# Gated cross attention with a mixture of experts: relative and causal terms of the edge tiles on PE instead of DVE and GpSimd

## The reference

```
x = x + tanh(g_xattn) * attention(ctx, ctx, layernorm(x))     # x: 4 x 1024 x 256, ctx: 4 x 154 x 256, 16 heads of 16
x = x + tanh(g_ffn)   * experts(layernorm(x))                 # 8 experts of 128, 4 chosen by token, and a shared one

# attention, for one batch and head; queries q = 0..1023, keys k = 0..153
scores = (qh @ kh.T) + bias[q, clip(q - k, -4, 4) + 4]        # bias = qh @ p_params
scores = where(q >= k, scores, -1e30)
out    = softmax(scores) @ vh                                  # then @ Wo.T
```

## Time and profile before

| | |
|---|---|
| median of 3 runs | 729.9 us (727.46 to 731.66) |
| profiled execution | 729.36 us, span 727.3 us |
| PE busy | 617.1 us, 85% of the span |
| DVE, ACT, POOL busy | 458.1, 275.9, 177.3 us |
| first score of the attention | 61.9 us |
| last unit of the attention starts | 334.1 us |
| experts' dense stretch starts | 393.9 us |
| mean granted TensorE clock | 0.938 |

### The profile page before, as it was taken

How to read it: one execution, slowest core, us unless ns; L and a number is a source line. 1 busy time by engine, 2 the same in 40 slices (tenths; PEclk the granted TensorE clock), 3 DMA queues, 4 the chain that set the end, 5 groups by cost and what they waited for, 6 DMA issues and landing times.

```text
span 727.3 us, 10637 instructions
## 1 busy us (share of the span) xinstructions
PE 617.1 (85%) x3384; PEld 484.7 (67%) x3384; DVE 458.1 (63%) x884; ACT 275.9 (38%) x501; POOL 177.3 (24%) x177
## 2 busy tenths in 40 slices
PE   3665968797977977878667999999999999999997
PEld 2544734566544755554345888888888888888886
DVE  3577657868387768751277575756557475755653
ACT  2433356334643465334351322333242333324222
POOL 2151005300341006100010232232324223232222
PEclk9966989999999999889959999999999999999999
DMA  7750233524144333473122112031222202121220
GB/s 235 209 122 23 45 75 87 124 50 98 39 116 93 74 82 84 110 211 99 31 47 82 37 60 86 2 102 43 87 58 73 72 5 97 43 87 59 74 73 29
DMA packets 39856, 58.65 MB, mean 81 GB/s; under 512 B 7984, under 2 KB 21040, under 8 KB 39792
## 3 DMA queue, kind: packets, MB, share of 16 engines
q1 hardware_dynamic: 39824, 58.25, 29.3%
HBM read 31.76 MB, written 4.85 MB: 50 GB/s over the span
## 4 chain that ended last, share of the span: by engine, by line
issue 44%; POOL 5%; PE 1%; DVE 1%; POOLq 0%; ACT 0%; DVEq 0%
POOL hl L1165 4%; PE work L948 1%; POOL rstd L1159 0%; DVE stats L1246 0%; PE py L1462 0%; POOLq L1163 0%; DVE x L1346 0%; DVE xn L1256 0%; POOL veps L1157 0%; PE oT L937 0%; PE oT L933 0%; DVE mv L1250 0%; DVE at L671 0%; POOLq L1164 0%; POOLq L1156 0%
## 5 line engine op out<-in xcount | busy, mean ns | idle before, releaser
L1165 POOL TENSOR_TENSOR hl<-sg,hh 128x512 fp32r<-128x512 f32 x72 | 93.1, 1293 | 249.0 <-ACT hh L1208 249.0
L503 ACT ACTIVATE ex<-sT 128x512 f32<-128x512 f32 (+1 forms) x160 | 91.9, 593 | 157.2 <-PE sT L913 132.6
L1202 ACT ACTIVATE sg<-pg 128x512 f32<-128x512 f32 x72 | 43.0, 597 | 199.0 <-PE pu L1447 198.2
L872 PE MATMUL smax<-km,qs 96*128 96x308 f32 (+1 forms) x244 | 86.9, 392 | 26.7 <-DVE mx L604 19.3
L604 DVE TENSOR_REDUCE mx<-smax 128x2 f32<-128x308 f32 x185 | 81.1, 472 | 36.3 <-PE smax L872 35.1
L872 PEld LDWEIGHTS smax<-km,qs 96*128 96x128 f32 x244 | 49.0, 211 | 60.5 <-DVE mx L604 34.0
L1462 PE MATMUL py<-wxl,hh 128*128 128x256 f32 x288 | 81.8, 284 | 3.3 <-DVE x L1346 2.1
L1462 PE MATMUL py<-wxh,hl 128*128 128x256 f32 x288 | 80.8, 281 | 0.0
L1462 PE MATMUL py<-wxh,hh 128*128 128x256 f32 x288 | 80.5, 280 | 0.0
L1334 DVE TENSOR_TENSOR sg<-cwb,sg 128x512 f32<-128x512 f32 x64 | 66.9, 1045 | 10.8 <-DMA cwb<-cwt_d 7.9
L1329 DVE TENSOR_TENSOR sg<-pu,sg 128x512 f32<-128x512 f32 x72 | 49.2, 684 | 28.3 <-ACT sg L1202 27.0
(11 more groups left out here) (154 smaller groups left out, 1120.7 us busy)
## 6 DMA issues: line engine op xcount, KB each, us to landing
cwb<-cwt_d SPq DMA_DIRECT2D x64, 256.0 KB, 3.4
qs<-qh SPq DMA_DIRECT2D x64, 128.0 KB, 2.5
qs<-ql SPq DMA_DIRECT2D x32, 128.0 KB, 2.6
at<-rden_d SPq DMA_DIRECT2D x64, 64.0 KB, 2.3
out<-x SPq DMA_DIRECT2D x8, 512.0 KB, 4.4
ks<-km SPq DMA_DIRECT2D x16, 231.0 KB, 3.6
wx<-in_wx SPq DMA_DIRECT2D x9, 384.0 KB, 5.8
x<-in_x SPq DMA_DIRECT2D x3, 1024.0 KB, 9.2
```

Source lines behind the costliest of these rows:

```text
L503: nc.scalar.activation(ex[:, g % 2, i % 5, q0:HALF], ST[i % 2][:, q0:HALF], ACT.Exp).then_inc(exp_s, 1)
L872: last_one = nc.tensor.matmul(bank[:, 0:width], qs[0:96, s, tile * P:(tile + 1) * P], km[:, s, 0:width], start=True, stop=True)
L1165: nc.gpsimd.tensor_tensor(hl[:, i % R, :], sg[:, i % R, :], hh[:, i % R, :], ALU.subtract).then_inc(hl_done, 1)
L1202: nc.scalar.activation(sg[:, i % R, :], PG[i % RG][:], ACT.Silu).then_inc(sg_s, 1)
```

## The change

- **Relative and causal terms on PE.** POOL makes `d0`, `d1` and the table `d0s` (the last four keys of tile 0) in two parts each, a rounded one and its remainder. PE adds them by matmuls with the identity: to the untransposed scores before the maxima, and to the transposed scores in the h = 0 unit. Copies to `sx`, DVE's adds, maxima and subtractions on it, and PE's transposes out of it are gone.
- **Relative terms by themselves.** Sixteen matmuls of 8 columns into two banks (`REL`, place 3 of the order) replace the extra columns. ACT copies these two banks to `relc`.
- **All maxima from PSUM**, 32 banks for each half, and one DMA of 512 queries in both halves.
- **A new order.** `PASS` seeks tiles 2 and 3 first, then tile 1, then tile 0; `SEEK` says how many places each step takes. The maxima are transposed in step 15 (h = 0) or 17 (h = 1), and ACT, not SP, issues their DMA. Keys move to steps 1 to 4, the split of the keys (`k_hi`, `k_lo`) to steps 14 to 16, the projection to steps 18 and 19.
- **`divide` moves from DVE to POOL**, behind the tables.
- **124 instead of 128 keys** in the long chunks, 30 instead of 26 in the short ones.
- **Start and handover.** The keys are split in thirds at the start, the second half of x is loaded before wv, and POOL divides the last unit.

```diff
-    X_USE, V_USE, Q_USE, K_USE, M_USE, Y_USE = (0, 11), 2, (3, 13), 5, (8, 15), (9, 16)
+    FIRST_USE, K_USE, X_USE, V_USE, Q_USE, M_USE, Y_USE = (0, 11), 0, (3, 11), 5, (6, 13), (8, 15), (9, 16)
+    PASS = (((2, 0), (2, 1), (3, 0), None, (3, 1), (2, 2), (2, 3), (3, 2), (3, 3),
+             (1, 0), (1, 1), (1, 2), (1, 3), (0, 0), (0, 1), (0, 2), (0, 3)),
+            ((0, 0), (0, 1), (1, 0), (1, 1), (2, 0), (2, 1), (0, 2), (0, 3),
+             (1, 2), (1, 3), (2, 2), (2, 3), (3, 0), (3, 1), (3, 2), (3, 3)))
+    SEEK = ((1, 1, 1, 1, 2, 2, 1, 0, 1, 1, 1, 1, 0, 1, 1, 2), (1, 1, 1, 1, 1, 2, 1, 1, 1, 2, 2, 1, 1))
+    M_STEP = (15, 17)
...
         def near(b, start):
...
+            pool.wait_ge(relc_s, 2 * (b + 1))
...
+            banded(d1[0][:], relr_h, 1, "band1", 32)
+            nc.gpsimd.tensor_tensor(d1[0][:], d1[0][:], con("causal1").unsqueeze(1).broadcast_to([P, H, 32]),
                                     ALU.add).then_inc(d_s, 1)
+            banded(d1[1][:], relr_l, 1, "band1", 32)
+            banded(d0[0][:], relr_h, 0, "band0", P)
+            banded(d0[1][:], relr_l, 0, "band0", P)
...
+        def near_ready(b, p):
+            if p == first_of(1):
+                pe.wait_ge(d_s, ND * b + 3)
+            if p == first_of(0):
+                pe.wait_ge(d_s, ND * (b + 1))
+        def stack_scores(b, h, q, bank):
+            if is_rel(h, q):
+                for s in range(NSTK):
+                    last_one = nc.tensor.matmul(bank[:, 2 * DIST * s:2 * DIST * (s + 1)],
+                                                qs[0:96, s, tile * P:(tile + 1) * P], km[:, s, PAIR:SW],
+                                                start=True, stop=True)
...
             if tile == 0:
+                for add in (cmask[:, 0:P].unsqueeze(1).broadcast_to([P, 2, P]), d0[0][:, 2 * s:2 * s + 2, :],
+                            d0[1][:, 2 * s:2 * s + 2, :]):
+                    last_one = nc.tensor.matmul(both[:, :, 0:P], idr[:], add, start=False, stop=True,
+                                                skip_group_check=True)
+            elif tile == 1:
+                for part in d1:
+                    last_one = nc.tensor.matmul(both[:, :, KM:KL], idr[:], part[:, 2 * s:2 * s + 2, 0:K1],
+                                                start=False, stop=True, skip_group_check=True)
...
         def score(b, h, step, start):
...
+            def add(q, keys, corrections):
+                for part in corrections:
+                    last = nc.tensor.matmul(out[0:keys, q], part, idr[:, q.start % P:(q.stop - 1) % P + 1], start=False,
+                                            stop=True, skip_group_check=True)
             if i < 4:
+                last_one = nc.tensor.matmul(out[0:KM, :], ks[:, s, j * KL:j * KL + KM],
+                                            qs[:, s, h * HALF:(h + 1) * HALF], start=True, stop=True)
                 if h == 0:
-                    for k in range(2):
-                        nc.tensor.transpose(out[:, k * P:(k + 1) * P], sx[:, k, s, j * KL:j * KL + P], ident)
+                    last_one = add(slice(0, P), KM, [cmask[:, 0:KM]] + [part[:, 4 * g + i, 0:KM] for part in d0])
             else:
...
                 if h == 0:
+                    add(slice(KM, P), P, [part[:, heads, :] for part in d0s])
+                    last_one = add(slice(P, 2 * P), P, [part[:, heads, :] for part in d1])
...
         def unit(b, h, carry, ahead):
...
+                if ahead and h == 1 and REL in sought(0, i):
+                    rel_out(b + 1)
+                if i == M_STEP[h] and (h == 0 or ahead):
+                    m_stack(b + h, 1 - h)
-                if ahead and h == 0 and i == 19:
-                    k_hi(b + 1, False)
+                if ahead and h == 0 and i in (14, 15):
+                    k_hi(b + 1, (i - 14,))
...
         def unit(b, h, carry, ahead):
...
             if h == 1 and ahead:
                 near(b + 1, False)
+            if carry:
+                divide(u - 1, 1 - h)
...
         def unit(b, h, carry, ahead):
...
+                for p in sought(mh, i):
+                    if h == 0 or ahead and p != REL:
+                        maximum(mb, mh, p)
-                if i in DIVIDE[h] and carry:
-                    divide(u - 1, 1 - h, (DIVIDE[h].index(i),))
-                if diagonal and i in TILE0:
-                    tile0(b + 1, TILE0.index(i))
```

More of the change, by code:

```diff
@@ L25 @@
 DIST = 4
+KM = P - DIST
+K1 = KL - KM
+ND = 7
 E, I = 8, 128
@@ L321, in unit @@
                 q_stack(h, 0)
+            if h == 1 and ahead:
+                k_stack(2)
             if h == 0 and not ahead:
@@ L479, in q_out, with rel_out, m_stack @@
                 nc.scalar.copy(qh[:, c, :], W[(use + c) % 2][:]).then_inc(q_hi, 1)
-        def near(b, p, banks=MAX_BANKS):
-            for k in range(2):
-                q = 2 * p + k
-                act.wait_ge(sm_ps, 4 * NM * b + q + 1)
-                nc.scalar.copy(sx[:, m_tile(0, p), m_stacks(p).start + k, :], banks[q % len(banks)][:, 0:SW])\
-                    .then_inc(sx_s, 1)
+        def rel_out(b, banks=MAX_BANKS):
+            if not (isinstance(b, int) and b == 0):
+                act.wait_ge(d_s, ND * b)
+            for tile in range(2):
+                q = 2 * REL + tile
+                act.wait_ge(sm_ps, PER_PASS * b + q + 1)
+                nc.scalar.copy(relc[:, tile * H:(tile + 1) * H, :].rearrange("p h d -> p (h d)"),
+                               banks[q % len(banks)][:, 0:H * DIST]).then_inc(relc_s, 1)
+        def m_stack(b, h):
+            act.wait_ge(mT_s, 2 * b + h + 1)
+            act.dma_start(qs[96:128, :, h * HALF:(h + 1) * HALF].bitcast(F32),
+                          mt[:].unsqueeze(1).broadcast_to([32, NSTK, HALF]).bitcast(F32)).then_inc(ms_in, 16)
         def raw_out(u, h, g):
@@ L869, in stack_scores @@
-        def stack_scores(tile, p, k, bank):
-            width = SW if tile < 2 else PAIR
-            s = m_stacks(p).start + k
-            last_one = nc.tensor.matmul(bank[:, 0:width], qs[0:96, s, tile * P:(tile + 1) * P], km[:, s, 0:width],
+                pe.wait_ge(mx_s, PER_MAX * b + 2 * NM * h + reduced(h, q - RING + 1))
+            if h == 0 and k == 0:
+                near_ready(b, p)
+            stack_scores(b, h, q, MAX_BANKS[q % RING])
+        def near_ready(b, p):
[3 more added lines that the diff above has]
+                pe.wait_ge(d_s, ND * (b + 1))
@@ L981, in tensor @@
+                if carry and i in ((19,) if h == 1 and not ahead else (18, 19)):
+                    for pr in (range(2) if h == 1 and not ahead else (i - 18,)):
+                        project(b - 1 + h, 1 - h, pr, b, Y_USE[h] + pr)
         transposes(0, -1, START)
         queries(-1, START, START + 2)
-        pe.wait_ge(kv_in, 3 * 16)
+        pe.wait_ge(wk_in, 16)
         keys(0, -1, START + 4)
+        pe.wait_ge(kv_in, 2 * 16)
         values_in(0, -1, START + 7)
         transposes(1, -1, START + 8)
-        pe.wait_ge(pool_set, 5)
```

475 lines of the change are left out of this document (221 added, 254 removed).

## The result

The changed kernel takes 753.8 us in the median of 4 runs (748.0 to 757.8), the kernel before 729.2 in the same session: a ratio of 1.032 (95% interval 1.027 to 1.036), slower by 3.2%. The forecast was 712 us. The profiled execution took 748.0 us and was the fastest of the four.

A forecast was written before the change was run, and what follows sets the result against it. PE was taken as the bound while it runs, with 72 us of idle and slow clock in seven units. -72 + 24.1 + 37.2 - 5.6 - 1.5 + 0 = -17.8 us gave 711.6, median 712; range 696 to 728.

The forecast's parts named there:

- The ring stop: Inside the h = 1 unit, PE's 3.66 us wait for DVE's reduction of a ring bank was to go.
- tables come late: Rival, chance 0.13: POOL slowed by DVE or relative banks 3 us later, steps 8 and 13 wait 3 us more; 725 us.
- the stop of 2.3 us for POOL's tables: At step 8 of the h = 1 unit, PE waits about 2.3 us for tile 1's tables.
- the stop at the end: At the end of the h = 1 unit, PE waits up to 1 us for the DMA of the maxima.
- The drain: Busy time before a stop counts 0.16 us of matmul drain as work; it goes with the stops, 5.6 us over seven units.
- The adds: Added PE work at 0.11 us a small add: 5.1 us per h = 0 unit, 5.6 per h = 1 unit, 37.2 together.
- small adds cost what their weight loads last: Rival, chance 0.08: each of 352 small adds costs 0.16 us or more; at 0.20, 744 us.
- The h = 0 units: Idle and slow clock left: 6 us in (0,0), 3 each in (1,0) and (2,0), 1.6 in (3,0).
- stops for ACT: In steps 13 to 16 of the h = 0 unit, PE waits 2.5 us for ACT.
- Start, handover and rest: First unit starts near 60.4 instead of 61.9 us, -1.5 us; the handover behind the last unit changes by 0.
- The median: The median of the runs lies 0.5 us above the profiled execution, making 711.6 into 712 us.
- The tables: POOL's tables in the h = 1 unit: tile 1's ready at 12 us, tile 0's at 20, no stop at step 13.

The follow-up runs named there:

- a_act_xn: The changed kernel with the four normalised tiles of the h = 1 unit written by ACT instead of DVE: 738.4 us, ratio 1.015.
- a_wide_first: The changed kernel with POOL's 2048-wide high table of tile 0 moved ahead of tile 1's tables, beside DVE's tiles: 763.4 us, ratio 1.046.
- a_turn: The changed kernel with POOL's relative tables in the h = 1 unit waiting until DVE has written the four normalised tiles: 751.6 us, ratio 1.032.
- a_act_merged: a_act_xn with the causal mask added into the high table by POOL instead of by matmuls of its own: 743.1 us, ratio 1.019.
- a_exact: a_act_xn with the h = 0 unit's normalised tiles in two pairs and the divisions of (3,1) on DVE: 732.0 us, ratio 1.003.
- a_act_late: a_act_xn with the experts' weights loaded only after the DMA of the last maxima has landed: 736.4 us, ratio 1.011.
- b_early: The kernel before with the h = 0 unit's maxima sought from step 0 and transposed in step 17: 731.9 us, ratio 1.006.

## Why the prediction was wrong

Against its own sum (711.6 us for the profiled execution, 748.0 measured, 36.4 us more), by its own steps:

**The ring stop, 18.8 us.** The step that failed is "nothing of 2 to 4 us stands ahead of it: the 3.66 us stop goes". Four `xn` of 3.34 us stand ahead of it. The three h = 1 units lost 29.3 us to idle and slow clock (6.9 + 4.9, 4.9 + 3.3, 5.8 + 3.4) where 10.5 were left to them. Shown by `a_act_xn`, where they lose 5.3, 2.6 and 2.9, and by `a_wide_first`. The mistake behind it was in reading: the prediction took 4.37 us as the length of two divisions and moved them to POOL as the cure. They were short instructions waiting for POOL; the change put 14 us of tables on POOL, earlier in the unit, beside another DVE instruction that takes turns with it. The rival "tables come late" had POOL slowed by DVE; here it was DVE that waited, and the tables came late only when `a_turn` made POOL wait.

That the three units of `a_act_xn` lose 10.8 us in all, so near to 10.5, is in part luck: the stop of 2.3 us for POOL's tables that the prediction left in each unit is 0.4 at most, while the stop at the end is 1.5, 1.15 and 1.5 us instead of up to 1, and (0,1) has one of 1.5 us for the DMA of the queries (`qs<-qh`, 1.53 in the changed kernel), which no step of the prediction has.

The Trainium skill (SBUF — State Buffer, section "Who interferes with whom") says that DVE and GpSimd share a pair of SBUF ports, held by one instruction until it ends, which concerns DVE's `tensor_scalar` in its two-port modes and its instructions with two SBUF inputs. This case agrees: 0.41 us became 3.79 beside 3.64. No view shows in which mode `xn` ran. The same section says that reductions don't contend, and ACT not either; here eight reductions, which read PSUM, took 3.18 us (0.40 each) while POOL worked in `a_act_merged`, and ACT's tiles in `a_act_xn`, with POOL's tables beginning beside them, took 0.59 to 0.60 each (twelve in all). With that rule the 4.37 us could have been read as a wait before the fact.

**The drain, 5.6 us.** "0.16 per stop is counted as work and goes with it" gave nothing. Work at full clock was forecast as 200.2 + 37.2 - 5.6 = 231.8 and came to 240.9; by unit it matches the price of the adds without this correction (39.05 for (1,0), where 33.8 + 5.1 make 38.9). So here the busy time before a stop was not work that went with the stop.

**The adds, 3.5 us more than 37.2.** The price of 0.11 us was right. PE's timeline after:

```profile
87.07 0.23 PE L932 MATMUL sT<-idr,cmask 128*124 128x128 f32 x1
87.14 0.27 PE L932 MATMUL sT<-idr,d0h 128*124 128x128 f32 x1
87.25 0.27 PE L932 MATMUL sT<-idr,d0l 128*124 128x128 f32 x1
87.35 0.63 PE L894 MATMUL smax<-km,qs 96*128 96x308 f32 x3
```

0.07, 0.11 and 0.11 from start to start. The rival "small adds cost what their weight loads last" falls. The Trainium skill (TensorE: Matmul & The Clock Gate, section "Back-to-back issue gap") has about 81 ns a pair, which is too low for these: the three take 0.10 us on average. Most of the extra lies in (0,0) and (3,0), whose work grew by 6.8 and 6.1 us instead of 5.1, and I have no row that says why.

**The h = 0 units, 4.4 us.** 18.0 us of loss instead of 13.6. The ends came as forecast (no wait for the maxima, stops for ACT of 1.0 to 1.2 where 2.5 was forecast), but the 1.4 us of `xn`, not in the working, made a stop in three units; in `a_exact` 0.95, 0.73 and 0.74 us of it are left. In (3,0) the loss of 4.3 instead of 1.6 us is the DMA beside the weights; `a_act_late` showed the cause, and that curing it there only moved the wait.

**Start, handover and rest, 4.2 us.** The first unit began at 62.6 instead of 60.4; the handover took 60.9 instead of 59.8 us, POOL's two divisions lasting 2.48 where DVE's lasted 1.29; behind it and around the span lie 0.9 more. 18.8 + 5.6 + 3.5 + 4.4 + 4.2 = 36.5, the 36.4 but for rounding.

**The median.** The prediction put it 0.5 us above the profiled execution; it lies 5.8 above. No trace shows where these 5.3 us of the miss lie.

**The tables** were nearly on the forecast: tile 1's done 13.6 us after the unit's start (forecast 12), tile 0's at 21.2 (20). They held nobody up: in the changed kernel the ring stop had already held PE, and without it, in `a_act_xn`, the stop for them was 0.4 us at most.

Even with the ring stop gone the forecast would not have stood. In the seven units of `a_act_xn` 31.4 us of idle and slow clock are left of 72, a gain of 40.6, and 43.0 us of work have come: nearly equal. `a_exact`, with the stops of the h = 0 units halved too, ends at 732.0. So the stop is about half of the 3.2% by which the change was slower (1.5% are left in `a_act_xn`); that the change is no gain even without it lies in the other terms. What stays open: why `b_early`'s hidden DMA gives nothing back, of which the lower clock in (1,1) and (2,0) is seen and not explained, and why the handover of `a_act_xn` is 2.3 us longer (63.2) than the changed kernel's: 1.3 us of it are its last projection at a granted clock of 0.56 instead of 0.73 (6.66 instead of 5.37 us), 0.4 the wait before it, and why the clock differs there no row says.

## What to carry to other kernels

Before a long duration of DVE is taken as the price of its work, look up the same instruction elsewhere in the trace: 0.69 us in one unit and 4.37 for two in another was a wait inside the instruction, which no list of waits shows. When POOL gets work, ask which DVE instructions on SBUF will lie beside it, and move those to ACT or away in time; a wait that only settled who goes first moved the stop here. A saving in stops must be set against the added work with nothing subtracted that a row does not show: here, at best, 41 us of stops gone met 43 us of added work.

## What the runs showed of the hardware

- A DVE instruction of 0.41 us (128x256, SBUF to SBUF, one tensor input) lasted 3.79 us beside a POOL instruction of 3.64; two of 0.69 with two SBUF inputs lasted 4.37 beside one of 3.61. POOL's instruction, the first to come, was no longer for it; where DVE's division came first, POOL's copy of 64 columns lasted 0.70 instead of 0.23. DVE's reductions from PSUM (0.40) and ACT's tiles (0.59 to 0.60 each) kept their pace.
- A DMA of 512 KB landed in 10.7 us where nine of 384 KB were issued around it on another engine's queue; in `a_act_late`, where the nine waited, all eight DMAs of maxima landed in 4.3 to 5.6.
- Matmuls with the identity, 124 or 128 weight columns and 4 to 128 moving ones, start 0.11 us apart, the first of a group 0.03 to 0.07 before the second (some of 128 columns 0.14 to 0.15); in the whole kernel one costs 0.07 to 0.11 us.
